# Self-attention of a Perceiver layer: batch 0's scores first, batch 1's projections between the probability turns

## The reference

```python
x = x + xattn(ctx_1024, layernorm(x), mask, ...)   # 16 heads of 64 over 2048 + 128 keys per batch
x = x + attn(layernorm(x), qw, kw, vw, ow)
x = x + ffn(layernorm(x), ...)                      # dense 512 -> 2048 -> 512, and product-key experts

def attn(x, qw, kw, vw, ow):                        # 2 x 128 x 512, 16 heads of 32
    Q, K, V = x @ qw, x @ kw, x @ vw
    Q, K = rope(Q, freq), rope(K, freq)             # pairs of neighbouring columns are rotated
    score = einsum('bhqd,bhkd->bhqk', Q, K) / sqrt(32)
    score = score - 1e10 * (1 - causal)
    weights = softmax(score - max(score))
    attn = einsum('bhqk,bhkd->bhqd', weights, V)
    return merged(attn) @ ow
```

## Time and profile before

| | us |
|---|---|
| median of three runs | 902.45 (900.21 to 902.87) |
| the profiled execution, device time | 903.4 |
| its span in the profile | 901.6 |
| PE busy in the span | 855.2 |
| DVE busy | 581.5 |
| ACT busy | 437.5 |
| POOL busy | 349.0 |

### The profile page before, as it was taken

How to read it: one execution, slowest core, us unless ns; L and a number is a source line. 1 busy time by engine, 2 the same in 40 slices (tenths; PEclk the granted TensorE clock), 3 DMA queues, 4 the chain that set the end, 5 groups by cost and what they waited for, 6 DMA issues and landing times.

```text
span 901.6 us, 17320 instructions
## 1 busy us (share of the span) xinstructions
PE 855.2 (95%) x6297; PEld 800.6 (89%) x6297; DVE 581.5 (64%) x1540; ACT 437.5 (49%) x1017; POOL 349.0 (39%) x362
## 2 busy tenths in 40 slices
PE   3999999999999999999999999999998789998997
PEld 2899999999999999999999999999878689996885
DVE  7455557566577877665565666777766347755885
ACT  4575554554556564545446464445416024334652
POOL 5723634534464656446454523333002010003442
PEclk9999999999999999999999999999996779999999
DMA  5446336465466677675655656877577255932310
GB/s 189 167 155 199 134 107 233 177 241 218 177 233 239 218 256 259 215 254 189 245 183 211 233 189 229 329 272 259 192 282 336 77 214 218 375 135 95 113 48 24
DMA packets 71110, 183.04 MB, mean 203 GB/s; under 512 B 6337, under 2 KB 19569, under 8 KB 65009
## 3 DMA queue, kind: packets, MB, share of 16 engines
q1 hardware_dynamic: 70928, 181.90, 56.5%
q10 hardware_dynamic: 96, 0.02, 0.0%
HBM read 130.00 MB, written 50.86 MB: 201 GB/s over the span
## 4 chain that ended last, share of the span: by engine, by line
PE 81%; DVE 8%; issue 4%; ACT 3%; DMA 2%; POOL 1%; SPq 0%; DVEq 0%; ACTq 0%; POOLq 0%
PE pJ L1621 14%; PE pJ L1623 14%; PE pJ L1622 14%; PE pV L1751 7%; PE pS L1729 4%; PE pT L1737 3%; PE pS L1737 3%; PE pT L1729 2%; PE pS L1621 2%; PE pS L1623 2%; PE pS L1622 2%; PE pX L1652 1%; DVE late L1578 1%; PE pV L1621 1%; DMA WS<-w_split 1%
## 5 line engine op out<-in xcount | busy, mean ns | idle before, releaser
L1621 PE MATMUL pJ<-WV,XT 128*128 128x256 f32 x544 | 158.6, 292 | 0.1
L1622 PE MATMUL pJ<-WV,XT 128*128 128x256 f32 x544 | 153.8, 283 | 0.0
L1623 PE MATMUL pJ<-WV,XT 128*128 128x256 f32 x544 | 153.7, 283 | 0.0
L848 ACT ACTIVATE SP<-SP,xneg 128x768 f32<-128x768 f32 (+1 forms) x96 | 85.8, 895 | 120.1 <-DVE xneg L1200 120.1
L1621 PE MATMUL pJ<-XT,WK 128*128 128x384 f32 (+1 forms) x384 | 126.9, 331 | 3.8 <-DVE VT L1096 2.8
L1623 PE MATMUL pJ<-XT,WK 128*128 128x384 f32 (+1 forms) x384 | 125.2, 326 | 0.0
L1622 PE MATMUL pJ<-XT,WK 128*128 128x384 f32 (+1 forms) x384 | 125.1, 326 | 0.0
L1096 DVE TENSOR_TENSOR KT<-pJ,KT 128x384 fp32r<-128x384 f32 x96 | 51.0, 534 | 88.9 <-ACT KT L825 88.5
L1621 PEld LDWEIGHTS pJ<-WV,XT 128*128 128x128 f32 x544 | 104.1, 191 | 0.8 <-DVE KT L1096 0.3
L1622 PEld LDWEIGHTS pJ<-WV,XT 128*128 128x128 f32 x544 | 104.2, 192 | 0.0
L1623 PEld LDWEIGHTS pJ<-WV,XT 128*128 128x128 f32 x544 | 104.0, 191 | 0.0
(11 more groups left out here) (364 smaller groups left out, 2189.3 us busy)
## 6 DMA issues: line engine op xcount, KB each, us to landing
WS<-w_split SPq DMA_DIRECT2D x14, 2048.0 KB, 8.7
WV<-wv_split SPq DMA_DIRECT2D x20, 1024.0 KB, 7.5
WK<-wk_split SPq DMA_DIRECT2D x40, 512.0 KB, 4.4
w_split<-wkst SPq DMA_DIRECT2D x40, 512.0 KB, 3.3
w_split<-wvst SPq DMA_DIRECT2D x40, 512.0 KB, 4.0
XA<-w_split SPq DMA_DIRECT2D x4, 2048.0 KB, 12.7
xraw<-in_ctx SPq DMA_DIRECT2D x7, 768.0 KB, 5.5
wk_split<-WK SPq DMA_DIRECT2D x8, 512.0 KB, 4.0
```

Source lines behind the costliest of these rows:

```text
L848: ac.activation(SP[:, I % 2, h, 0:w], SP[:, I % 2, h, 0:w], ACT.Exp, bias=xneg[:, I % 2, h:h + 1], scale=XSC, accum_out=total).then_inc(c_ ...
L1621: te.matmul(dst, a(HI), b(HI), start=start, stop=False)
L1622: te.matmul(dst, a(HI), b(LO), start=False, stop=False)
L1623: return te.matmul(dst, a(LO), b(HI), start=False, stop=stop)
```

## The change

On PE, QR's turn of batch 0 moves behind `project_rows(1, 0)`, V's projection of batch 0 is cut into two halves with the turns of KR (batch 0) and of `hnA` (batch 1) between them, and `scores(0)` follow directly. Batch 1's projections come after that, and between them stand the turns and value products of groups 0 to 2; V's projection of batch 1 is cut in half as well. `scores(1)` come after `weigh_values(2)`. The first matmuls of `mix_rows(0)` move ahead of the turn of AO (batch 1). The turned probabilities of groups 0 to 3 all go into one bank, and ACT instead of DVE copies them; groups 4 to 7 alternate between two banks and are copied by DVE. ACT's and DVE's lists follow the new order. Banks of batch 0's values and of batch 1's Q, K and V change places. The lists of SP and POOL do not change. No instruction is added or removed.

```diff
-        TBANK = (pJ[:, 0, :], pJ[:, 0, :], pT[:, 1, :], pX, pX, pV, pX, pV, pX, pV)
+        TBANK = (pJ[:, 0, :], pT[:, 1, :], pX, pJ[:, 0, :], pJ[:, 1, :], pV, pX, pV, pX, pV)
+        PBANK = (pJ[:, 0, :],) * 4 + (pJ[:, 1, :], pJ[:, 0, :]) * 2
...
-                ac.activation(VV[:, b, :], (pT[:, 0, :], pJ[:, 0, :])[b], ACT.Copy).then_inc(s_vh, 1)
+                ac.activation(VV[:, b, :], (pV[:, :], pT[:, 0, :])[b], ACT.Copy).then_inc(s_vh, 1)
...
+            def probs_copy(g):
+
+                act.wait_ge(s_pt2, g + 1)
+                ac.activation(PV2[:, g % 4, :], PBANK[g], ACT.Copy).then_inc(s_p2h, 1)
+
             joined_hi(ITERS - 2)
             transposed_hi(HT, 0)
             joined_hi(ITERS - 1)
+            transposed_hi(QTs, 0)
+            transposed_hi(KN, 0)
             transposed_hi(HT, 1)
-            transposed_hi(QTs, 0)
             values_hi(0)
-            transposed_hi(KN, 0)
             exps(0)
             exps(1)
+            probs_copy(0)
+            exps(2)
+            probs_copy(1)
+            transposed_hi(QTs, 1)
+            exps(3)
+            transposed_hi(KN, 1)
+            probs_copy(2)
             values_hi(1)
-            transposed_hi(QTs, 1)
-            transposed_hi(KN, 1)
-            for g in range(2, 8):
+            probs_copy(3)
+            for g in range(4, 8):
                 exps(g)
...
-                z = ((pS[:, 0, :], pS[:, 1, :]), (pV, pJ[:, 1, :]))[b][m]...
+                z = ((pS[:, 0, :], pS[:, 1, :]), (pJ[:, 1, :], pV))[b][m]...
...
-                ve.tensor_copy(PV2[:, g % 4, :], pJ[:, (g + 1) % 2, :]).then_inc(s_p2h, 1)
+                ve.tensor_copy(PV2[:, g % 4, :], PBANK[g]).then_inc(s_p2h, 1)
...
             dve.wait_ge(d_rope, 48)
+            rotate(0, 0)
             add_rows(0, 1)
-            rotate(0, 0)
+            rotate(1, 0)
             norm_rows(0, 1)
+            transposed_lo(QTs, 0)
+            transposed_lo(KN, 0)
             transposed_lo(HT, 1)
-            transposed_lo(QTs, 0)
-            rotate(1, 0)
+            row_max(0)
+            row_max(1)
+            row_max(2)
             rotate(0, 1)
-            transposed_lo(KN, 0)
+            row_max(3)
             rotate(1, 1)
-            for g in range(4):
-                row_max(g)
             transposed_lo(QTs, 1)
             transposed_lo(KN, 1)
-            probs_copy(0)
-            probs_copy(1)
-            row_max(4)
-            row_max(5)
-            probs_copy(2)
-            probs_copy(3)
-            row_max(6)
-            row_max(7)
+            for g in range(4, 8):
+                row_max(g)
+            probs_copy(4)
             norm_outputs(0)
-            probs_copy(4)
             probs_copy(5)
-            transposed_lo(AT, 0)
             probs_copy(6)
             probs_copy(7)
+            transposed_lo(AT, 0)
             norm_outputs(1)
+            transposed_lo(AT, 1)
             add_rows(1, 0)
-            transposed_lo(AT, 1)
...
-            def project_rows(m, b):
+            def project_rows(m, b, ks=range(4)):
...
-                bank = ((pS[:, 0, :], pS[:, 1, :], pT[:, 0, :]), (pV[:, :], pJ[:, 1, :], pJ[:, 0, :]))[b][m]
-                rows(bank, HT, b, 2 + m).then_inc(s_wuse if b == 1 else s_qkv, 1)
+                bank = ((pS[:, 0, :], pS[:, 1, :], pV[:, :]), (pJ[:, 1, :], pV[:, :], pT[:, 0, :]))[b][m]
+                for k in ks:
+                    last = product(bank, lambda s: HT[:, s, k, L * b:L * b + L], lambda s: slot4(2 + m, s)[:, k, :], k == 0, k == 3)
+                if 3 in ks:
+                    last.then_inc(s_wuse if b == 1 else s_qkv, 1)
 
             def scores(b):
 
-                if b == 0:
-                    pe.wait_ge(s_vh, 1)
-                else:
+                if b == 1:
+                    pe.wait_ge(s_vh, 2)
                     pe.wait_ge(s_sm, 4)
-                pe.wait_ge(s_tl, 4 + 2 * b)
+                pe.wait_ge(s_tl, 3 + 3 * b)
...
             def turn_weights(g):
 
+                if 1 <= g < 4:
+                    pe.wait_ge(s_p2h, g)
+                if g >= 5:
+                    pe.wait_ge(s_p2h, g - 1)
                 pe.wait_ge(s_se, g + 1)
-                if g == 0:
-                    pe.wait_ge(s_rope, 4)
-                elif g == 1:
-                    pe.wait_ge(s_vh, 2)
-                else:
-                    pe.wait_ge(s_p2h, g - 1)
                 for h in range(4):
-                    last = te.transpose(pJ[:, (g + 1) % 2, P * h:P * h + P], SM[:, g % 4, P * h:P * h + P], ident[:, :])
+                    last = te.transpose(PBANK[g][:, P * h:P * h + P], SM[:, g % 4, P * h:P * h + P], ident[:, :])
...
             def weigh_values(g):
...
+                pe.wait_ge(s_vh, b + 1)
                 pe.wait_ge(s_p2h, g + 1)
...
-            def mix_rows(b):
+            def mix_rows(b, ks=range(4)):
...
             project_rows(1, 0)
-            project_rows(2, 0)
-            turn_rows(hnA, 1, s_src, 2)
             turn_rows(QR, 0, s_rope, 1)
-            pe.wait_ge(s_tl, 2)
             pe.wait_ge(c_mg, ITERS)
-            project_rows(0, 1)
+            project_rows(2, 0, (0, 1))
             pe.wait_ge(c_scl, 4 * PAIRS)
             turn_rows(KR, 0, s_rope, 2)
+            turn_rows(hnA, 1, s_src, 2)
+            project_rows(2, 0, (2, 3))
+            scores(0)
+            pe.wait_ge(s_tl, 4)
+            project_rows(0, 1)
+            turn_weights(0)
+            pe.wait_ge(s_vh, 1)
             project_rows(1, 1)
-            scores(0)
-            project_rows(2, 1)
             turn_rows(QR, 1, s_rope, 3)
+            turn_weights(1)
+            weigh_values(0)
+            pe.wait_ge(s_sm, 4)
+            project_rows(2, 1, (0, 1))
             turn_rows(KR, 1, s_rope, 4)
-            turn_weights(0)
-            turn_weights(1)
-            scores(1)
-            weigh_values(0)
+            turn_weights(2)
             weigh_values(1)
-            turn_weights(2)
+            project_rows(2, 1, (2, 3))
             turn_weights(3)
             weigh_values(2)
+            scores(1)
             weigh_values(3)
             turn_weights(4)
-            turn_rows(AO, 0, s_ao, 1)
             turn_weights(5)
             weigh_values(4)
+            turn_rows(AO, 0, s_ao, 1)
+            turn_weights(6)
             weigh_values(5)
-            turn_weights(6)
             turn_weights(7)
             weigh_values(6)
             weigh_values(7)
-            mix_rows(0)
+            mix_rows(0, (0,))
             turn_rows(AO, 1, s_ao, 2)
+            mix_rows(0, (1, 2, 3))
```

More of the change, by code:

```diff
@@ L1365, in rotate @@
                     dve.wait_ge(s_wuse, m + 3)
-                z = ((pS[:, 0, :], pS[:, 1, :]), (pV, pJ[:, 1, :]))[b][m].rearrange("p (h e two) -> p h e two", h=SH, two=2)
+                z = ((pS[:, 0, :], pS[:, 1, :]), (pJ[:, 1, :], pV))[b][m].rearrange("p (h e two) -> p h e two", h=SH, two=2)
                 r = (QR, KR)[m][:, b, :].rearrange("p (h e two) -> p h e two", h=SH, two=2)
@@ L1918, in weigh_values @@
                 last.then_inc(s_pv2, 1)
-            def mix_rows(b):
+            def mix_rows(b, ks=range(4)):
                 pe.wait_ge(s_tl, 7 + b)
                 weight_ready(5)
-                rows(OUT2[b][:, :], AT, b, 5).then_inc((s_y, s_wuse)[b], 1)
+                for k in ks:
+                    last = product(OUT2[b][:, :], lambda s: AT[:, s, k, L * b:L * b + L], lambda s: slot4(5, s)[:, k, :], k == 0, k == 3)
+                if 3 in ks:
+                    last.then_inc((s_y, s_wuse)[b], 1)
             turn_rows(hnA, 0, s_src, 1)
```

## The result

The changed kernel takes 896.35 us, the median of 20 runs (893.81 to 900.03); the kernel before, beside it, 901.53 us, the median of 20 (896.33 to 907.27). The ratio is 0.9943, its 95% interval 0.9926 to 0.996: faster by 5.2 us, where 9.1 were forecast. The 893.5 us of the forecast is missed by 2.9, inside its range of 889 to 899.

The account below looks back on a forecast made before the run. TensorE's own work was taken to set the pace, at half clock in self-attention; 7.0 + 1.5 - 0.4 + 1.0 = 9.1 us off 903.4 gave 894.3, less 0.95 for the median, taken as 893.5 us, range 889 to 899.

Parts of the forecast that it names:

- (a) to (e): Self-attention up to mix_rows(0): the new order starts mix_rows(0) at 698.2, 7.0 us before 705.19.
- (d): Behind weigh_values(3): PE waits 2.1 us before turn 4, then 0.6 for exps(5); clock falls there, about 685.5.
- (e): Groups 4 to 7 at half clock: four turns 3.6 and four products 7.1, 10.8 us to mix_rows(0).
- The rule weighed in the prediction: Full clock does not engage for transposes: six turns cost 0.45 more each, 6.4 us gained instead of 9.1.
- Rival 1: Clock falls among mixed turns, products and half projections: 5.6 us gained (896.9) or 2.1 (900.4); chance 0.15.
- (f): mix_rows(0) split around AO's turn: the 1.48 wait before mix_rows(1) goes, 1.5 us gained; norm_rows(1,0) gives back 0.4.
- (g): Two half-clock stretches from the queries on, covering 4.8 and 3.4 us: 1.0 us earlier, between -0.7 and 2.7.

Follow-up runs that it names:

- block: Changed kernel with batch 1's three projections in one block, turns and products of groups 0 to 3 behind them: 898.46 us, ratio 0.998 to the kernel before.
- the repeat: The changed kernel run and profiled once more, nothing altered: 896.3 us, ratio 0.995 to the kernel before.
- lite: Changed kernel plus 12 idle matmuls, 8 behind weigh_values(3) and 4 behind group 4's turn: 891.53 us, ratio 0.989 to the kernel before.
- look3: The kernel before, unaltered, profiled once more: 896.46 us, an execution of its lower group.
- mixwhole: Changed kernel with mix_rows(0) whole ahead of AO's second turn, as before the change: 895.96 us, against 896.3 of the changed kernel.
- tailonly: Changed kernel plus 27 idle matmuls, 16 and 5 around hn's second turn, 6 behind the queries: 891.79 us, ratio 0.9888 to the kernel before.
- fillhn: fill plus 16 idle matmuls in the 4.56 us wait ahead of hn's second turn: 889.64 us, ratio 0.9896 to the kernel before.
- beforefill: The kernel before plus 29 idle matmuls, in its waits and between turns and products: 895.59 us, ratio 0.9959 to the kernel before.
- fill: Changed kernel plus 22 idle matmuls, from behind weigh_values(3) to among the later turns and products: 892.33 us, ratio 0.9911 to the kernel before.

## Why the prediction was right, and where it fell short

**(a) to (e), to mix_rows(0), are right, the last term in part by luck.** Counted from the first turn, scores(0) stand at 15.8 (forecast 15.5), scores(1) at 31.25 (30.7), group 4's turn at 35.8 (35.2), mix_rows(0) at 47.35 (47.5). The new wait of (d) is 2.00 and 0.71, where 2.1 and 0.6 were worked out, and ACT ends it. The product at full clock, which no row had, takes 0.81 a group (0.89 taken, 1.78 as the other end). The cover of groups 0 to 3 held: no wait for a copy between their turns. Block shows what it is worth, one wait of 0.85 for a copy and one of 0.84 for `row_max`. But group 4's turn came 0.6 late, and from group 5's turn to mix_rows(0) it took 9.9 (689.41 to 699.32) where (e) says 10.8: a group's product at half clock takes 1.57 here (690.29 to 691.86), and my 1.78 was too much. Two errors cancel.

**Where the clock falls, and why.** It fell at 688.0, 36.1 behind the first turn, and in the repeat 34.7 behind it, where (d) has 34.8: at the wait of 2.00 both times, as forecast. Lite shows that the work behind is not what loses it: with the waits filled, the same turns and products ran at full clock to the mixes and beyond. The rule weighed in the prediction, from the Trainium skill, "TensorE: Matmul & The Clock Gate", section "Part 4: PE-mode transpose", doesn't hold for the lists of this kernel: four turns take 0.44 at full clock between half a projection and a product, and in look3 the clock came back among turns and products. Rival 1, that it falls among the mixed work, did not happen, and not even block brought it about, which took the dense halves out from between; so those are not what kept it from happening.

**(f) was 0.7 too large in the first profile, and its reason was wrong.** 0.8 came of its 1.5. I let the clock return 4.4 us behind mix_rows(0)'s start; it took 5.8, and 1.4 us more at half clock is 0.7. In the repeat it took 4.6, and mix_rows(1) began 5.9 behind mix_rows(0), where (f) has 5.8: the size was within what the clock moves from run to run, the reason was not. The split itself is worth nothing, as mixwhole shows, though (f) put the whole gain on the covered copies: norm_rows(1,0) on DVE is next late in either order. I had named it, and let it give back 0.4, but of a split that alone gave 1.5; in mixwhole the hn turn waits for it all the same.

**(g), the later clock, was 1.0 and came to 0.3.** In the repeat it was -2.4. The second stretch was 3.4 us long, as I took it; the first covers 5.3 us of the queries and not 4.8 (0.25 more lost), and a dip at 814.3 came that the kernel before doesn't have. Single dips of 3.4 us come and go, each worth at most 1.7 us, and one profile can't price them. Each stands at a wait for DVE, and the same wait is also seen without one. All 14 profiles have a wait of 1.74 that ends between 804 and 820: 8 show a dip in it or within 1.5 us behind it, 6 don't. All have a wait of 1.5 to 2.1 near 46: 2 show a dip. At 736 the repeat has a wait of 1.77 and a dip, and block one of 1.66 and none. The first profile of the changed kernel had that dip, at 46.3, and its stage began 1.3 later. That filling waits keeps this clock too is what tailonly shows: around hn's second turn and behind the queries lie some 5 us, which the prediction took as given. Filling the wait of 4.56 alone (fillhn) was not enough for it.

**The baseline was too high.** This is the rest of the shortfall. The sum was made against an execution of 903.4, with 0.95 taken off for the median, and the three runs I had all lay in the upper group. Of the 20 runs beside the changed kernel 7 lie below 899, and look3, one execution of that kind, shows why: the clock is back 13.8 us earlier (695.6 against 709.4), so that the half clock that the change saves was never paid there. So the gain is 6.3 by the two profiles and 5.2 by the medians. The 3.9 us between 9.1 and 5.2 are 0.7 from (f), 0.7 from (g), 1.3 ahead of the stage and 1.1 from the baseline; the last 0.1 is the others together.

**Two mechanisms, not one.** The forecast told of a stage with a shorter way and a clock that falls later, and both are shown. At held clocks the new order's stage is 4.8 shorter (3.2 at least, with the idle matmuls evened out). The clock alone is worth 5.3 in the old order (beforefill) and 4.0 to 5 in the new one (fill, lite), with the price of the idle matmuls taken off. The change took only part of the second: it moved the fall from 682 to 688.0, and of 27.3 us at half clock up to the mixes it left 17.1. Against the kernel before as in look3, which has 13.7 there, it takes nothing of it.

**What stays open.** Why the clock comes back at 695.6 in some executions of the kernel before and at 709 in others. The four profiles have the same work in the same order, and the clock moves against it: it falls 31.5, 31.5, 32.1 and 33.4 us behind the first turn, and only the third has the early return. Four are too few to say which offset brings which return, and no run set it on purpose. Nor is it known why the same wait near 46 or 815 is followed by a dip in some executions and not in others.

## What to carry to other kernels

A dependency wait of TensorE costs its own length and can cost the clock behind it, so price both; where it can't be covered by real work, try idle matmuls on operands that lie ready (12 of them gained about 5 us here, 49 some 9). Put them into the wait first: 12 there did as well as 22 of which ten stood among the work behind. Reordering for cover is worth the waits that it hides: find what is late next before a split is put down as a gain. When the runs of a kernel fall into two groups, profile it until both are seen, and forecast against each: here the change gains 5.8 us on one and about 1 on the other.

## What the runs showed of the hardware that was not expected

- 49 idle matmuls, about 11 us of TensorE, made the kernel 9 us faster than the changed one. The Trainium skill, "TensorE: Matmul & The Clock Gate", section "Why this matters for your kernels", advises against gaps in which TensorE is idle between bursts; the runs agree, and add that gaps of 2.00 and 0.71 us between small matmuls were where the clock fell here.
- A gap doesn't always cost the clock: with a wait of 0.84 ahead of the last projection, and behind it 9 us of nothing but turns, products, scores and a wait of 0.85, block held the full clock until its wait of 2.00. And one and the same wait of 1.74 near 815 is followed by a dip in some executions only.
- Returns are not bound to dense work. In look3 the clock came back while PE did 128-column turns and 32-column products; the sixteen records of two groups went from 3.62 to 2.07 and 1.97.
- The kernel before spreads over 11 us (896.33 to 907.27) and the changed one over 6 (893.81 to 900.03), in 20 runs each. The mean granted clock of a run goes with it: 0.976 to 0.984 in the 20 of the changed kernel, 0.976 to 0.986 in the 29 of the kernel before beside the repeat. A change of order alone changed how far the time of a kernel varies.
